# Two attention layers in one kernel: half of a step's background projections moved ahead of its second score

## What is computed

```python
def _lora_linear(x, W, A, B):
    return x @ W + SCALING * (x @ A @ B)
# layer 0: 32 query heads, 8 key/value heads, no mask
q, k, v = lora(hidden), lora(traces), lora(traces)
scores = einsum('bhqd,bhtd->bhqt', q, k) / sqrt(HD)
context = einsum('bhqt,bhtd->bhqd', softmax(scores), v)
hidden = hidden_states + _lora_linear(context, Wo, Ao, Bo)
# layer 1: 32 heads of its own keys and values, a mask over the keys, then a layer norm
scores = where(mask, einsum(q, k) / sqrt(HD), -inf)
x = hidden_states + (softmax(scores) @ v) @ Wo.T + bo
return (x - mean(x)) / sqrt(var(x) + 1e-05) * ln_g + ln_b
```

## Time and profile before

| | |
|---|---|
| median of 3 runs | 1941.54 us (1935.04 to 1947.71) |
| the profiled execution's own time | 1943.69 us |
| its span in the trace | 1941.9 us |
| mean granted TensorE clock | 0.968 |
| TensorE busy | 1760.9 us (91%) |
| VectorE busy | 1268.2 us (65%) |
| ScalarE busy | 994.1 us (51%) |

### The profile page before, as it was taken

The page is one execution under the profiler, slowest core; times in us unless marked ns, Lnnn a source line. Parts: engine busy times, 40 slices in busy tenths (PEclk is TensorE's granted clock), DMA queues, the critical chain, the costliest instruction groups (busy, mean ns, idle before and its releaser), DMA issues.

```text
span 1941.9 us, 43752 instructions
## 1 busy us (share of the span) xinstructions
PE 1760.9 (91%) x18340; PEld 1114.8 (57%) x18340; DVE 1268.2 (65%) x2743; ACT 994.1 (51%) x1880; POOL 186.8 (10%) x268
## 2 busy tenths in 40 slices
PE   6699997999999999998999999999999899998985
PEld 3456544565555654554566566666666566665652
DVE  2566665666667777765755667767776677767751
ACT  0055554555555555554544555545555455555562
POOL 2010211001210001011101100001000100001001
PEclk8799998999999999998999999999999999999996
DMA  7911325113352222134242436323543235334300
GB/s 193 237 47 27 78 61 155 28 35 68 73 153 44 44 44 53 26 98 129 61 70 62 93 44 121 54 40 52 95 80 47 39 59 117 46 41 64 47 8 11
DMA packets 65029, 138.12 MB, mean 71 GB/s; under 512 B 12540, under 2 KB 49436, under 8 KB 64832
## 3 DMA queue, kind: packets, MB, share of 16 engines
q1 hardware_dynamic: 64832, 135.33, 34.4%
HBM read 97.84 MB, written 34.89 MB: 68 GB/s over the span
## 4 chain that ended last, share of the span: by engine, by line
PE 80%; DVE 6%; ACT 6%; issue 3%; DMA 3%; POOL 2%; SPq 1%; POOLq 0%; ACTq 0%
PE value L756 21%; PE work L664 11%; PE work L644 10%; PE score L733 9%; PE ring L713 8%; PE score L738 8%; DVE chunk_max L923 4%; PE work L689 4%; PE work L787 3%; ACT p_sb L822 3%; PE ring L701 2%; DMA q_stack<-few_rows 2%; ACT v_sb L844 1%; ACT full L833 1%; PE ring L766 1%
## 5 line engine op out<-in xcount | busy, mean ns | idle before, releaser
L822 ACT ACTIVATE p_sb<-score 124x512 f32<-124x512 f32 (+1 forms) x1664 | 904.9, 597 | 794.1 <-PE score L733 410.1
L923 DVE TENSOR_REDUCE chunk_max<-ring 128x1 f32<-128x402 f32 x2048 | 1065.7, 569 | 362.6 <-PE ring L713 354.2
L713 PE MATMUL ring<-k_stack,q_stack 64*128 64x402 f32 x2048 | 739.1, 426 | 58.3 <-DVE chunk_max L923 45.3
L756 PE MATMUL value<-p_sb,v_sb 124*32 124x256 f32 x6656 | 451.9, 394 | 0.0
L713 PEld LDWEIGHTS ring<-k_stack,q_stack 64*128 64x128 f32 x2048 | 353.5, 187 | 123.5 <-DVE chunk_max L923 97.1
L733 PE MATMUL score<-q_stack,k_stack 64*124 64x512 f32 (+1 forms) x832 | 321.9, 474 | 28.7 <-DMA q_stack<-few_rows 26.4
L738 PE MATMUL score<-q_stack,k_stack 64*124 64x256 f32 (+1 forms) x1664 | 309.7, 311 | 22.0 <-ACT p_sb L822 21.5
L738 PEld LDWEIGHTS score<-q_stack,k_stack 64*124 64x124 f32 (+1 forms) x1664 | 212.4, 184 | 119.4 <-ACT p_sb L822 62.2
L756 PEld LDWEIGHTS value<-p_sb,v_sb 124*32 124x32 f32 x6656 | 180.6, 111 | 169.4 <-issue 81.8
L644 PE MATMUL work<-ctx_sb,wk 64*128 64x402 f32 x1280 | 261.8, 512 | 17.4 <-DMA ctx_sb<-ctxT 7.0
L664 PE MATMUL work<-wv,ctx_sb 64*124 64x128 f32 x3840 | 264.2, 274 | 11.6 <-ACT v_sb L844 6.9
(11 more groups left out here) (67 smaller groups left out, 556.4 us busy)
## 6 DMA issues: line engine op xcount, KB each, us to landing
k_stack<-k_dram SPq DMA_DIRECT2D x288, 200.1 KB
k_dram<-k_parts SPq DMA_DIRECT2D x60, 402.0 KB, 2.8
ctx_sb<-ctxT SPq DMA_DIRECT2D x24, 992.0 KB, 6.7
k_dram<-k_parts SPq DMA_DIRECT2D x20, 395.0 KB, 2.6
q_stack<-few_rows SPq DMA_DIRECT2D x256, 2.0 KB
wq<-l_Wq SPq DMA_DIRECT2D x2, 1024.0 KB, 9.7
xt_sb<-xT SPq DMA_DIRECT2D x4, 512.0 KB, 11.0
wo<-l_Wo SPq DMA_DIRECT2D x2, 1024.0 KB, 7.2
```

Of the source, the lines that this page charges most:

```text
L713: engine.matmul(ring[bank_of["max", n]][:, 0:MW], q_stack[rows, u % 3, j, q * P:(q + 1) * P], k_stack[rows, 2 * (z % 3) + (u % 2 if u < L0 ...
L756: done = engine.matmul(value_bank[32 * j:32 * j + 32, 0:S], v_sb[0:tn, seq % 2, i, head * VW:head * VW + 32], p_sb[0:tn, (2 * n + j % 2) % ...
L822: engine.activation(p_sb[0:tn, n % PLACES, :], score_bank[n % 2][0:tn, :], ACT.Exp, scale=SCALE).then_inc(s_exp, 1)
L923: engine.tensor_reduce(chunk_max[:, u % 2, half, j * QT + q, c:c + 1], ring[bank_of["max", n]][:, 0:MW], AX.X, ALU.max).then_inc(s_taken[" ...
```

## The change

One call of `background(rate / 2)` moves from behind the pair of maxima to between the first score's maximum and the second score. The amounts stay: the list of steps has the same 7055 entries, and each of the 832 steps holds the same ones; in 452 of them they stand in another order. In 338 of these, pieces now stand on both sides of the second score. The pair of maxima of step 12 becomes the last thing in its step.

```diff
@@ -355,12 +355,12 @@
                 self.step("score", u, i, 0)
                 if self.max_turn < goal:
                     self.max_chunk()
+                self.background(rate / 2)
                 self.step("score", u, i, 1)
                 if self.max_turn < goal:
                     self.max_chunk()
                 self.background(rate / 2)
                 self.max_pair(goal)
-                self.background(rate / 2)
                 if i == 3 and u % UB == 0 and u > 0:
                     self.step("bias att", u // UB - 1)
```

## The result

The changed kernel takes 1967.07 us (median of 4 runs, 1966.49 to 1969.27) against 1939.82 for the kernel before (median of 4, 1935.04 to 1947.71). The ratio is 1.0138, 95% interval 1.0103 to 1.0174: **slower by 1.4%, 27 us**. The profiled execution took 1966.49 us, 22.8 more than the one of before; its span is 1964.7 us, at a granted clock of 0.969. The two traces thus explain 23 of the 27 us, which is within the interval.

A forecast was written before the change was run, and what follows sets the result against it. PE's order and waits were taken as the bound, ACT's turn-round as the other limit. 5.4 + 10.1 + 6.0 - 7.0 = +14.5 us gave 1958.2 for the profiled execution, 2.15 above the median, so 1956.0 us; range 1934 to 1982.

The forecast's parts named there:

- the four places of loss and gain: Fewer pieces behind the second score +5.4 us, unit ends +10.1, product starts +6.0, product ends -7.0.
- the case of no effect: Rival: PE's later waits at DVE's ring and the maxima's DMA swallow the terms; time stays 1941.5 us; chance 0.09.
- (3): Unit ends: pair of maxima directly ahead of the next unit's first two, four in a row; +10.1 us, between 5 and 14.
- (1): About 78 steps, k piece before and after the second score: later second exponential, nothing gained or lost, margin 0.02 us.
- (2): Steps with fewer pieces behind the second score: the next second score comes later; +5.4 us.
- (4): 30 steps, product's first piece ahead of the second score while its banks are still read: second pair follows it; +6.0 us.
- (5): 46 steps, product ends ahead of the second score: earlier reading, gains of 0.11 (k) and 0.26 (v); -7.0 us.
- The slow rival: Free steps with pieces on both sides: second exponential becomes the bound, +30 us, 1986 us; chance 0.20.
- The term that I had put at nothing: Additional switches between pieces and scores cost nothing; 0.05 us in each of 338 steps would be 17 us.
- The sign to look for: If the prediction is right, PE's idle time behind reductions of maxima rises from 45.3 us.
- The fast one: Rival: PSUM readings hide behind unrelated pieces in every free step; 26 us less, 1915.5 us; chance 0.09.

The follow-up runs named there:

- Kernel 9: The changed kernel, but in steps 1 and 5 all pieces stay behind the second score; ratio 1.0099 against the kernel before.
- Kernel 1: The kernel before, with only the pair of maxima of step 12 moved to the end of its step; ratio 1.0089.
- kernels 2: The kernel before, with only the pieces moved ahead of the second score, the pair of maxima keeping its place; ratio 1.0100.
- 11: The kernel before, with pairs of maxima in steps 3, 7 and 12, between pieces, and half the pieces ahead of the second score; ratio 0.9801.
- Kernel 4: The changed kernel, but a product is never started ahead of the second score; ratio 1.0207 against the kernel before.
- Kernel 5: The changed kernel, but readings of products ending ahead of the second score stand behind that score again; ratio 1.0289 against the kernel before.
- kernel 3: The changed kernel, but full-row pieces of a single last v tile never go ahead of the second score; ratio 1.0127 against the kernel before.
- kernel 10: The kernel before, with the pairs of maxima in steps 3, 7 and 12 instead of 4, 8 and 12; 1868.52 us, ratio 0.9628.

## Why the prediction was right, and where its sizes were off

The direction, the four places of loss and gain, and the range held; the size was half: 14.5 us forecast, 27 measured (20 to 34 by the interval), 23 between the traces. The measured 1967 us lies above 1960.9, so it is "slower by over 1%", to which I had given 0.33, and not within 1%, to which I had given 0.58. The range was wide enough to hold the case of no effect too, so that the number fell into it says less than the terms do. The 8.9 us that the traces lie above the sum are +2.7 from (3), +4.2 from (1) and (2), +2.2 each from (4) and (5), +6.8 for the full-row pieces, -4.5 for starts that gained, and -4.7 for the rest. Part of the errors cancelled, by luck.

- **(1), (2) later second exponential.** The chain was confirmed (1.39 for 1.40, 2.05 for 2.05), but the margin of 0.02 us in full steps, "nothing lost", was none: the value in step 2 came 0.07 later in unit 14, and 0.07 to 0.10 in most full steps 1 and 5 with k pieces; in steps 9 nothing was lost. In all, 129 steps with their successors lost 9.6 us instead of 5.4, 8.9 of it from steps 1 and 5; two odd places (units 4 and 27, step 1) hold 1.7 of that, for a reason that I don't know. Kernel 9 shows it by itself. The slow rival names this mechanism; it asked for 30 us more, and 4.2 came. By the prediction's own figures three v pieces and then two cost 0.13 and not 0.2, which changes little.
- **(3) the unit end.** Right in place and price (1.42 for 1.40 us). 12.8 instead of 10.1 us: 4.7 for 4.6 in the units with v pieces, at 0.25 in most of them, and 8.1 for 5.5 in those with k pieces. Kernel 1 alone costs 15 to 17. What I missed is that the maximum behind the delayed second score feeds the same queue (kernels 2, 11).
- **(4) starts under a reading.** +8.2 for +6.0 where the reading is right before: 0.19 to 0.25 us in 22 places, as forecast, but 0.47 to 0.55 in the other 9. In 30 further starts the step got shorter, -4.5, which I had not counted. Kernel 4 shows that the starts as a whole are a gain once ends stand early.
- **(5) ends ahead.** -4.8 for -7.0: v products as forecast (0.25 for 0.26), k products 0.02 in most places instead of 0.11. The k product's sum was off by itself: from the piece's start to the values rows 5 give 518.36 - 517.49 = 0.87 us, so with the second pair the values stand at 517.27 + 0.87 + 0.22 = 518.36, and the gain is nothing. Kernel 5 shows the dependence, 24 us.
- **The term that I had put at nothing**, and the largest single miss, is "so I take the additional switches between pieces and scores at nothing". It holds for half-row pieces and fails for the full-row ones: 6.8 us in 16 steps, shown by the traces and by kernel 3. The Trainium skill, page TensorEngine Tiling (Array Packing), section Key Properties, says that changing the tiling mode drains TensorE, while different tiles can run in parallel. This case's traces agree in time, though they don't show the drain itself: 0.62 us for one score and maximum between full-row matmuls, and 0.20 to 0.22 for the pair between half-row ones.
- **The sign to look for was hidden.** I had said that PE's idle time behind reductions would rise; it fell from 45.3 to 35.4 us. Taken step by step (idle times of over 0.1 us ahead of a maximum), it did rise in steps 0, from 2.1 us in 7 places to 5.2 in 22. But it fell from 29.9 to 18.7 in steps 4 and 8, where the second score now comes later and takes part of the fourth maximum's wait: in unit 14's step 8 that maximum waits 0.23 instead of 0.33 us, and the first value stands at 1.77 instead of 1.78, so nothing was gained.
- **The rivals.** The fast one, evacuation overlaps, is there in 49 places and is small. The Trainium skill's rule on rotating through PSUM banks, so that an evacuation overlaps the next group's matmuls (page Perfetto Trace Analysis, section Matmuls), gives the direction of kernel 10, where the reductions run under pieces, but not this change's. "No effect" fell. Whether the 4 us between the traces' 23 and the timed 27 are an effect stays open; the interval does not require them.

## What to carry to other kernels

Independent work between two instructions helps only if one of them waits for the other's result today; ask for each pair which wait ends there, before moving anything. In a ring of three banks count the producers that follow each other without other work and multiply by the consumer's interval: taking the pairs of maxima out of steps that had four in a row gave about 39 us, while moving a single one of them behind the values gave nothing. The other large part of kernel 10's 3.7%, about 30 us, came from a DMA issued a step earlier; ask what else a move makes earlier before you credit it to the wait that you had in mind. Read losses on a pipelined engine from distances between the same instruction's starts, not from its busy or idle time.

## What the hardware showed that I had not expected

A score and maximum on half the rows each, set between matmuls on all 128 rows, took 0.62 us, against 0.20 to 0.22 between half-row pieces; the steps grew by 0.42 to 0.44 in 16 places out of 16. A maximum (402 columns) alone between two value tiles, which use 32 columns of the array each, moved them from 0.46 to 0.94 us apart, and one alone behind the values cost 0.37, as much as two on the two halves together. And lost time is recorded as busy: the same 18340 matmuls took 1760.9 us of busy time in one order and 1782.1 in the other.
